# Softmax denominators of a second attention, inverted as 128 x 32 between two transfers, and another hand-over to the expert mixture

## The chip, the cores and the metric

The kernel runs on one core of one Trainium2 chip. The metric is the device time of one execution in microseconds (us). Before the change it is 692.34 us, the median of 3 runs (692.29 to 694.89).

## The reference, cut to what matters

The program is two gated blocks over x of shape (32, 64, 256): attention and feed-forward with 2:4 sparsity, then a second attention and a mixture of eight experts. The change is in the second attention and at its border with the mixture. In numpy-like words, per batch of 64 channels and 256 positions:

```
xn  = layernorm(x)                                  # over 256
qh, kh, vh = xn, ctx, ctx reshaped to (8 heads, 8 channels, 256)
qk  = einsum('bhdq,bhdl->bhql', qh, kh) / sqrt(8)   # 256 x 256 per head
ret = einsum('bhql,bhdl->bhdq', softmax(qk, -1), vh)
x   = x + tanh(g_xattn[1]) * gamma * ret
xn  = layernorm(x)
x   = x + tanh(g_ffn[1]) * (shared_expert(xn) + top2_of_8_experts(xn))
```

The softmax is written as exp(qk - max), its sum over l (the denominator), and one division of the mixed values by that sum. The mixture begins with `xn @ W_router` in plain float32, which chooses the experts.

## The kernel before, in words

`attention1` holds the second attention. x is cut into 16 tiles of 128 rows (two batches of 64 channels); a tile has 16 units (2 batches x 8 heads) of 8 channels. Five engine programs run side by side. Each calls `run_steps` with a function `step(s)`: step s works on several tiles, each at another stage: tile v = s-1 (scores and their row maxima), t = s-2 (transposed scores, exponentials, weighted sums), o = s-3 (the last quarter of the weighted sums, the denominators, the residual), and on VectorE (DVE) also p = s-4 (layernorm statistics of the new x). The first steps are written out, the middle is a hardware loop of two steps, the rest is written out; `LAG` (3) says how many steps come after the last tile has begun.

Within a step, TensorE (PE) goes through units u = 0 to 15. Each unit writes transposed scores of tile t into one of three banks `st_ps` (line 1312) and scores of tile v into one of three banks `s_ps` (line 1317). ScalarE (ACT) takes the exponential of each `st_ps` bank (L1215); DVE takes the maximum over each row of each `s_ps` bank (`TENSOR_REDUCE`, L1387). PE can begin unit u only when the bank of unit u-3 has been read. Weighted sums (`products`, L1270) go to `pv_ps`, and ACT copies them by quarters of a tile into `pv` (L1200). In `pv`, each group of 32 partitions holds, per unit, 8 rows of weighted values and on row 8 the denominators, because the value matrix `vt` has a column of ones.

At u = 5 and 7 PE multiplies `pv` by two 0/1 matrices (`selected`, L1285): `sel_out` collects the value rows into channel order, and `sel_den` copies each denominator row onto the 8 channels of its unit. ACT copies both halves, 128 x 512, into `back` (L1227, at u = 8). DVE inverts `back[:, 1]`, 128 x 256, in two halves of 128 columns (L1393, at u = 10 and 12). GpSimd (POOL) multiplies by the inverse and adds to x (L1172, L1174). DVE takes statistics (L1398).

The maxima go another way: DVE negates them, PE turns them (`turn`, L1254, at u = 2 for tile t and u = 11 for tile v), ACT copies (`a_neg_t`, L1194), and a DMA of 8 KB from SyncE's (SP's) queue puts them into the operands (`maxima`, L1095). SP's queue also carries the context tile (L1113), the operand loads (`load_operands`, L254 and L261), and the raw expert weights (L1080 to L1088), in the order of `step`. POOL prepares the next queries, splits expert weights and issues the stores of the queries (L219).

After the steps PE transposes the first four normalized tiles for the mixture (`turned.transpose`, L276), ACT copies and rounds them (L281, L286), and DVE forms their low parts (`turned.low`, L291). At the end of a block each engine drains and all meet at a barrier; in the trace this carries the line of the block's `ExitStack` (L667 for the end of the first feed-forward, L975 for the end of `attention1`). `mixture1` then loads the router weights (L1511) on SP, and PE's first work is `router(0)` on them (L1562), then the transposes of group 1 (L1548) and `router(1)`.

Of the kernel before, what the change touches and what calls it, by code (L numbers as in the profile page):

```python
# [5 lines left out]
F32 = mybir.dt.float32  # L6
# [7 lines left out]
P = 128  # L14
# [945 lines left out]
def attention1(nc, sem, keep, d):  # L960
# [14 lines left out]
    with ExitStack() as ctx:  # L975
        def sb(name, shape, dt):
# [16 lines left out]
        rden = sb("a1_rden", [P, D], F32)  # L993
# [8 lines left out]
        vt_done, vt_ready, sel_done, back_ready, rden_ready, att_ready, x_ready, st_ready = (  # L1002
            sem("a1_" + n) for n in ("vt_done", "vt_ready", "sel_done", "back_ready", "rden_ready", "att_ready", "x_ready", "st_ready"))
# [13 lines left out]
        LAG = 3  # L1017
        FILL = 18
        FIRST = Step(0, 0, 1)
# [32 lines left out]

        def opposite(u):

            return u ^ 1
# [12 lines left out]
        def _(sp):  # L1068
            def load_shared():
                for m, name in enumerate(("L1_ffn_Ws_gate", "L1_ffn_Ws_up")):  # L1070
                    sp.dma_start(ws_raw[:, m], a[name].rearrange("(c p) j -> p c j", p=P)).then_inc(ws_loaded, 16)
                down = a["L1_ffn_Ws_down"]
                sp.dma_start(wsd_raw[:, 0:FULL], down[0:FULL * P].rearrange("(c p) n -> p c n", p=P)).then_inc(ws_loaded, 16)
                sp.dma_start(wsd_raw[0:LASTM, FULL], down[FULL * P:DS]).then_inc(ws_loaded, 16)

# [31 lines left out]

            def step(s):
                maxima(s.plus(-2), 1)
                v = s.plus(-1)  # L1110
                if v.inside(TILES):
                    after(sp, vt_done, v.plus(-2))
                    sp.dma_start(ctx_t[:, v.slot], dram_at(d["ctx"], v.n)).then_inc(ctx_loaded[v.slot], 16)  # L1113
                load_operands(s, 0)
                maxima(s.plus(-1), 0)
                if s.inside(TILES) and not (s.known and s.n == 0):
                    load_pieces(s)
                load_operands(s, 1)
                if s.known and s.n == 0:
                    load_pieces(s)  # L1120
                    load_shared()
# [4 lines left out]
        def _(pool):  # L1126
# [7 lines left out]
            def step(s):  # L1134
                n, l, o = s.plus(-1), s.plus(-2), s.plus(-3)
# [33 lines left out]
                if o.inside(TILES):  # L1169
                    after(pool, rden_ready, o, 2)  # L1170
                    after(pool, x_ready, o.plus(-1))
                    pool.tensor_tensor(att[:], back[:, 0], rden[:], ALU.mult).then_inc(att_ready, 1)  # L1172
                    after(pool, att_ready, o)
                    pool.tensor_tensor(at(x_all, o.n), at(x_all, o.n), att[:], ALU.add).then_inc(x_ready, 1)  # L1174
# [8 lines left out]
        def _(act):  # L1183
# [3 lines left out]
            def step(s):  # L1187
                v, t, o = s.plus(-1), s.plus(-2), s.plus(-3)
# [12 lines left out]

                if s.known and s.n == TILES + LAG - 1:
                    norm.scalar(act, EARLY)
                for u in range(UNITS):
# [39 lines left out]
        def _(pe):  # L1244
            def step(s):
                v, t, o = s.plus(-1), s.plus(-2), s.plus(-3)
# [29 lines left out]
                def selected(w_, m):  # L1276
# [3 lines left out]
                    if m == 0:  # L1280
                        after(pe, pv_ready, w_, QUADS)
# [7 lines left out]

                def keep_active(count):  # L1290

                    for c in range(count):
                        pe.matmul(pv_ps[:], lhsT=kop[0][:, c % QUADS, 0:P], rhs=kop[0][:, 0:2].rearrange("p g n -> p (g n)"),
                                  start=True, stop=True)

                for u in range(UNITS):
# [34 lines left out]
                    if u in (5, 7):  # L1331
                        selected(o, (u - 5) // 2)
                    if u == 11:
                        def before():
                            after(pe, neg_t_ready, t, 2)
                            after(pe, back_ready, o)
# [14 lines left out]
            for dc in range(DC):  # L1351
                turned.transpose(pe, first_xn, dc, s_ps[dc][:], ident)

        @block.vector
        def _(dve):
# [6 lines left out]
            def step(s):  # L1362
                v, t, o, p = s.plus(-1), s.plus(-2), s.plus(-3), s.plus(-4)
# [11 lines left out]
                if s.known and s.n == TILES + LAG - 1:  # L1375
# [6 lines left out]
                for u in range(UNITS):  # L1382
# [21 lines left out]
def mixture1(nc, sem, keep, d):  # L1404
# [7 lines left out]
    with ExitStack() as ctx:  # L1412
# [12 lines left out]
        wr = sb("m_wr", [P, DC, E], F32)  # L1425
# [44 lines left out]
        wr_loaded, consts, xn_done = sem("m_wr_loaded"), sem("m_consts"), [sem(f"m_xn_done{g}") for g in range(GROUPS)]  # L1470
# [566 lines left out]
def flamingo(nc, a, out):  # L2037
# [13 lines left out]
    with ExitStack() as ctx:  # L2051
# [43 lines left out]
        keep["turned"] = Turned(sb, sem)  # L2095
        attention1(nc, sem, keep, d)
# [27 lines left out]
```

## Time and profile before

| | |
|---|---|
| median of 3 runs | 692.34 us |
| profiled execution, its own time | 690.52 us |
| its span, first to last instruction | 688.6 us |
| PE busy / weight loads | 599.5 us (87%) / 455.9 us (66%) |
| DVE busy | 507.8 us (74%) |
| ACT busy | 404.8 us (59%) |
| POOL busy | 315.0 us (46%) |
| second attention | from 259 to 500 us |
| mixture | from 500 us to the end |

Busy time counts instructions in execution; matmul ends are modelled, so PE's share is not PE at its peak. The granted clock ("PEclk") is that of TensorE: 1.00 is 2.4 GHz, 0.50 is 1.2 GHz. Times in a timeline are us from the span's start.

### The profile page before, as it was taken

Reading aid. Unit: us, or ns where it says so; the run is one execution under the profiler, and the core shown is the slowest. Engines: PE = TensorE matmul, PEld = TensorE weight load, DVE = VectorE, ACT = ScalarE, POOL = GpSimd, SP = SyncE. Lnnn points to the kernel's source line nnn. Section 1 sums busy time; section 2 is a strip of 40 time slices with the busy share of each in tenths; the row PEclk is TensorE's granted clock in tenths of the full one; section 3 lists DMA queues with packets and bytes.
Section 4 is the critical chain, followed back from the end, with each engine's and each line's share of the span. In section 5 each row is a group of like instructions: output and inputs, shape, how many; then the busy total and the mean of one; then the engine's idle time right before and its main releaser. Section 6 shows DMA issues by size and latency. Waiting matters only on the chain. (4 is left out here: it accounts for less than half of the span.)

```text
span 688.6 us, 16656 instructions
## 1 busy us (share of the span) xinstructions
PE 599.5 (87%) x4987; PEld 455.9 (66%) x4987; DVE 507.8 (74%) x1013; ACT 404.8 (59%) x829; POOL 315.0 (46%) x432
## 2 busy tenths in 40 slices
PE   4688878999999957999899899989579789999994
PEld 2577756788888855554455445444268679999873
DVE  2878885688887978689999999997536744444656
ACT  3888883444434423688888888888635235555431
POOL 2455554233322549556656565562144534124254
PEclk9999998999999985999999999999859999999999
DMA  5434449200000025334444433440001335456344
GB/s 162 114 102 129 122 122 314 93 1 1 0 0 1 24 70 169 101 111 140 121 118 124 132 114 113 133 121 28 1 0 50 125 96 184 147 149 189 123 137 124
DMA packets 68640, 70.70 MB, mean 103 GB/s; under 512 B 8404, under 2 KB 64852, under 8 KB 68596
## 3 DMA queue, kind: packets, MB, share of 16 engines
q1 hardware_dynamic: 63364, 55.84, 27.2%
q0 software_dynamic: 5232, 14.29, 6.7%
q8 instruction: 25, 0.41, 0.2%
q14 instruction: 19, 0.16, 0.1%
HBM read 38.48 MB, written 31.36 MB: 101 GB/s over the span
## 5 line engine op out<-in xcount | busy, mean ns | idle before, releaser
L1387 DVE TENSOR_REDUCE a_smax<-a_s 128x2 f32<-128x512 f32 x256 | 163.4, 677 | 13.9 <-PE a_s L1317 11.6
L1215 ACT ACTIVATE a_prob<-a_st 128x512 f32<-128x512 f32 x256 | 141.8, 596 | 37.3 <-PE a_st L1312 36.1
L1312 PEld LDWEIGHTS a_st<-qop,kop 64*128 64x128 f32 x512 | 70.8, 187 | 70.0 <-DVE a_smax L1387 40.8
L1312 PE MATMUL a_st<-qop,kop 64*128 64x256 f32 x512 | 104.2, 315 | 12.8 <-DVE a_smax L1387 12.8
L1317 PE MATMUL a_s<-kop,qop 64*128 64x256 f32 x512 | 106.5, 324 | 5.8 <-DVE a_smax L1387 3.6
L1270 PE MATMUL a_pv<-a_prob,a_vt 128*32 128x256 f32 x1024 | 81.6, 391 | 3.1 <-ACT a_pv_sb L1200 1.5
L819 POOL TENSOR_TENSOR f_hs_lo<-f_kept,f_hs_hi 128x512 fp32r<-128x512 f32 x32 | 41.3, 1323 | 85.6 <-ACT f_hs_hi L769 85.6
L1317 PEld LDWEIGHTS a_s<-kop,qop 64*128 64x128 f32 x512 | 73.0, 193 | 8.0 <-DVE a_smax L1387 4.9
L1832 POOL DMA_INDIRECT sorted_rows<-m_xn,m_slot x32 | 33.0, 1031 | 48.5 <-PE m_gu L128 25.9
L126 PE MATMUL f_bank<-f_xt_hi,w_hi 128*128 128x512 f32 x128 | 51.1, 400 | 1.2 <-DVE w_raw L865 0.6
L127 PE MATMUL f_bank<-f_xt_lo,w_hi 128*128 128x512 f32 x128 | 50.6, 395 | 0.0
L128 PE MATMUL f_bank<-f_xt_hi,w_lo 128*128 128x512 f32 x128 | 50.5, 394 | 0.0
L787 ACT ACTIVATE f_mag<-w_raw 128x512 f32<-128x512 f32 x32 | 20.2, 633 | 44.7 <-DVE w_raw L865 44.7
L126 PE MATMUL f_bank<-wd_hi,f_hs_hi 128*128 128x256 f32 x128 | 37.4, 292 | 6.3 <-POOL f_hs_lo L819 6.2
L1848 POOL DMA_INDIRECT m_xn<-expert_rows,m_slot x16 | 15.7, 984 | 55.0 <-DMA expert_rows<-turned 40.2
L1172 POOL TENSOR_TENSOR a_att<-a_back,a_rden 128x256 f32<-128x256 f32 x16 | 11.6, 727 | 57.8 <-DVE a_rden L1393 57.8
L865 DVE TENSOR_TENSOR w_raw<-f_sg,f_bank 128x512 f32<-128x512 f32 x32 | 21.9, 685 | 21.5 <-ACT f_sg L783 15.6
L127 PE MATMUL f_bank<-wd_lo,f_hs_hi 128*128 128x256 f32 x128 | 37.0, 289 | 0.0
L128 PE MATMUL f_bank<-wd_hi,f_hs_lo 128*128 128x256 f32 x128 | 36.9, 288 | 0.0
L1270 PEld LDWEIGHTS a_pv<-a_prob,a_vt 128*32 128x32 f32 x1024 | 20.6, 108 | 21.9 <-ACT a_pv_sb L1200 3.8
L1393 DVE RECIPROCAL a_rden<-a_back 128x128 f32<-128x128 f32 x32 | 29.9, 938 | 6.9 <-ACT a_back L1227 6.9
L783 ACT ACTIVATE f_sg<-f_bank 128x512 f32<-128x512 f32 x32 | 18.8, 586 | 27.0 <-PE f_bank L128 27.0
(260 smaller groups left out, 1663.4 us busy)
## 6 DMA issues: line engine op xcount, KB each, us to landing
qop<-qop_rows SPq DMA_DIRECT2D x64, 100.0 KB
kop<-kop_rows SPq DMA_DIRECT2D x64, 96.0 KB
sorted_rows<-x_all SPq DMA_DIRECT2D x2, 2944.0 KB, 15.4
qop<-sorted_rows SPq DMA_DIRECT2D x46, 128.0 KB, 2.3
expert_rows<-turned SPq DMA_DIRECT2D x46, 128.0 KB
kop_rows<-k_hi SPq DMA_DIRECT2D x32, 128.0 KB, 2.3
qop_rows<-q_hi POOLq DMA_DIRECT2D x30, 128.0 KB, 2.7
x_all<-in_x SPq DMA_DIRECT2D x4, 512.0 KB, 5.4
```

The costliest lines, as they stand in the source:

```text
L126: pe.matmul(out, lhsT=lh, rhs=rh, start=first, stop=False, **kw)
L127: pe.matmul(out, lhsT=lh, rhs=rl, start=False, stop=False, **kw)
L128: return pe.matmul(out, lhsT=ll, rhs=rh, start=False, stop=last, **kw)
L819: pool.tensor_tensor(hs[1][:, j], kept[:, j], raw(hs[0][:, j]), ALU.subtract).then_inc(hs_ready, 1)
L865: dve.tensor_tensor(hid[:, c, j], sg[:, j % 2], u_ps[j % 2][:], ALU.mult).then_inc(hid_ready, 1)
L1215: act.activation(prob[:, u % 8], st_ps[BANK[u]][:], ACT.Exp, scale=SCALE1).then_inc(prob_ready, 1)
L1270: mm = pe.matmul(pv_ps[v4 * 32:(v4 + 1) * 32, 0:D], lhsT=vt[:, w_.slot, c, u], rhs=prob[:, u % 8, c * D:(c + 1) * D], start=(c == 0), stop ...
L1312: st = pe.matmul(st_ps[BANK[u]][:, c * D:(c + 1) * D], lhsT=kop[t.slot][rows, u // 2, c * P:(c + 1) * P], rhs=qop[t.slot][rows, u // 2], s ...
L1317: sm = pe.matmul(s_ps[BANK[u]][:, c * D:(c + 1) * D], lhsT=qop[v.slot][rows, w // 2, c * P:(c + 1) * P], rhs=kop[v.slot][rows, w // 2], st ...
L1387: dve.tensor_reduce(smax[:, v.slot, opposite(u)], s_ps[BANK[u]][:].rearrange("p (q n) -> p q n", q=2), AX_X, ALU.max).then_inc(smax_ready, 1)
L1393: dve.reciprocal(rden[:, cols], back[:, 1, cols]).then_inc(rden_ready, 1)
L1832: pool.indirect_dma_start(out=d["sorted"][b], out_offset=bass.IndirectOffsetOnAxis(ap=slot[:, k, t:t + 1], axis=0), in_=xn[:, t], in_offse ...
```

## The change

- `back[:, 1]` is no longer inverted. Once `pv` of tile o is complete, a DMA (`spread`) takes its four denominator rows (4 partitions x 1024) to `den`, 128 partitions x 32. DVE inverts that in one instruction at u = 9 into `inverse`, and a second DMA (`collect`) writes the inverses over the denominator rows of `pv`. Both are issued on SP.
- `selected`, the copy to `back` and POOL's two instructions move one step later, to tile s-4; POOL multiplies by `back[:, 1]` as it comes. The statistics move to tile s-5, and `LAG` is 4.
- The last tile takes no transfers: its denominators go through `selected` as before, and DVE itself inverts 128 x 256, multiplies, adds and takes statistics.
- `turned.low` moves behind the statistics of the last tile. PE runs `WARM` = 10 matmuls of 512 columns without use after the transposes.
- The router weights are loaded in step 0 of `attention1`, behind the shared weights.

```diff
+        den = sb("a1_den", [P, UROWS], F32)
+        inverse = sb("a1_inverse", [P, UROWS], F32)
-        LAG = 3
+        LAG = 4
+        DRAIN = TILES + 2
+        WARM = 10
+        def last(t):
+            return t.known and t.n == TILES - 1
 # sync: load_shared, and the step
+                sp.dma_start(keep["wr"][:], a["L1_ffn_W_router"].rearrange("(c p) e -> p c e", p=P)).then_inc(keep["wr_loaded"], 16)
+            def den_rows(w_):
+                return pv[D1:P:UROWS, w_.slot].rearrange("p q n -> p (q n)")
+            def spread(o):
+                if o.inside(TILES) and not last(o):
+                    after(sp, pv_ready, o, QUADS)
+                    after(sp, inverse_ready, o.plus(-1))
+                    sp.dma_start(den[:], den_rows(o)).then_inc(den_spread[o.slot], 16)
+            def collect(o):
+                if o.inside(TILES) and not last(o):
+                    after(sp, inverse_ready, o)
+                    sp.dma_start(den_rows(o), inverse[:]).then_inc(inverse_stored[o.slot], 16)
             def step(s):
                 maxima(s.plus(-2), 1)
+                spread(s.plus(-3))
                 v = s.plus(-1)
...
                 load_operands(s, 0)
+                collect(s.plus(-3))
                 maxima(s.plus(-1), 0)
 # gpsimd
-                if o.inside(TILES):
-                    after(pool, rden_ready, o, 2)
-                    after(pool, x_ready, o.plus(-1))
-                    pool.tensor_tensor(att[:], back[:, 0], rden[:], ALU.mult).then_inc(att_ready, 1)
+                if p.inside(TILES) and not last(p):
+                    after(pool, back_ready, p)
+                    after(pool, x_ready, p.plus(-1))
+                    pool.tensor_tensor(att[:], back[:, 0], back[:, 1], ALU.mult).then_inc(att_ready, 1)
 # scalar
-                    if u == 8 and o.inside(TILES):
-                        after(act, sel_done, o)
-                        after(act, att_ready, o.plus(-1))
+                    if u == 8 and p.inside(TILES):
+                        after(act, sel_done, p)
+                        after(act, att_ready, p.plus(-1))
 # tensor: selected, the step, the end
-                        after(pe, pv_ready, w_, QUADS)
+                        if last(w_):
+                            after(pe, pv_ready, w_, QUADS)
+                        else:
+                            after_dma(pe, inverse_stored, w_)
+                        after(pe, back_ready, w_.plus(-1))
-                        selected(o, (u - 5) // 2)
+                        selected(p, (u - 5) // 2)
+            pe.wait_ge(pv_ready, TILES * QUADS)
+            keep_active(WARM)
 # vector
-                    if u in (10, 12) and o.inside(TILES):
-                        cols = slice((u - 10) // 2 * P, (u - 8) // 2 * P)
-                        after(dve, back_ready, o)
-                        after(dve, att_ready, o.plus(-1))
-                        dve.reciprocal(rden[:, cols], back[:, 1, cols]).then_inc(rden_ready, 1)
-                    if u == 2 and s.known and s.n == TILES + LAG:
-                        turned.low(dve, FIRST)
+                    if u == 9 and last(s.plus(-4)):
+                        o = s.plus(-4)
+                        after(dve, back_ready, o)
+                        after(dve, x_ready, o.plus(-1))
+                        dve.reciprocal(ctx_t[:, 0], back[:, 1]).then_inc(inverse_ready, 1)
+                        after(dve, inverse_ready, o)
+                        dve.tensor_tensor(att[:], back[:, 0], ctx_t[:, 0], ALU.mult).then_inc(att_ready, 1)
+                        after(dve, att_ready, o)
+                        dve.tensor_tensor(x_all[:, o.n], x_all[:, o.n], att[:], ALU.add).then_inc(x_ready, 1)
+                    elif u == 9 and o.inside(TILES) and not last(o):
+                        after_dma(dve, den_spread, o)
+                        after_dma(dve, inverse_stored, o.plus(-1))
+                        dve.reciprocal(inverse[:], den[:]).then_inc(inverse_ready, 1)
                     if u == 3 and p.inside(TILES):
                         after(dve, x_ready, p)
                         dve.bn_stats(at(norm.stats, p.n), at(x_all, p.n)).then_inc(st_ready, 1)
+                    if u == 4 and last(p):
+                        turned.low(dve, FIRST)
 # mixture1, sync
-            sp.dma_start(wr[:], a["L1_ffn_W_router"].rearrange("(c p) e -> p c e", p=P)).then_inc(wr_loaded, 16)
```

## Rows read from the trace of the kernel before

**Rows 1.** Busy time by stretch, one stretch of the second attention (columns as named)
```profile
core 0: us, PE busy (x) PEld busy (x) DVE busy (x) ACT busy (x) POOL busy (x), PEclk, DMA share, GB/s
404.00:417.00 13.00, 12.02 (x150) 6.58 (x150) 12.21 (x22) 10.75 (x24) 7.96 (x14) 1.00 0.41 119
```

**Rows 2.** Waits, 300 to 470 us: total us, times, longest
```profile
PE a_st L1312 <- DVE a_smax L1387: 11.5, 13, 1.0
DVE a_smax L1387 <- PE a_s L1317: 4.9, 13, 0.4
```

**Rows 3.** Groups of instructions, 240 to 490 us: busy us, mean ns, idle before
```profile
L1387 DVE TENSOR_REDUCE a_smax<-a_s 128x2 f32<-128x512 f32 x256 | 163.4, 677 | 13.9 <-PE a_s L1317 11.6
L1393 DVE RECIPROCAL a_rden<-a_back 128x128 f32<-128x128 f32 x30 | 28.1, 940 | 6.9 <-ACT a_back L1227 6.9
```

**Rows 4.** Timeline of PE, one tile: start us, us, idle before in brackets
```profile
408.80 0.38 PE L1312 MATMUL a_st<-qop,kop 64*128 64x256 f32 x1 [0.90 <-DVE a_smax L1387]
...
409.81 0.38 PE L1312 MATMUL a_st<-qop,kop 64*128 64x256 f32 x1
...
422.23 0.38 PE L1312 MATMUL a_st<-qop,kop 64*128 64x256 f32 x1 [0.92 <-DVE a_smax L1387]
```

**Rows 5.** Timeline of DVE in the same tile
```profile
418.70 0.93 DVE L1393 RECIPROCAL a_rden<-a_back 128x128 f32<-128x128 f32 x1
```

**Rows 6.** Timeline of ACT in the same tile, the last quarter of `pv`
```profile
413.10 0.39 ACT L1200 ACTIVATE a_pv_sb<-a_pv 128x256 f32<-128x256 f32 x1
```

**Rows 7.** Timeline of SP's issues in the same tile
```profile
413.39 0.36 SPq L1113 DMA_DIRECT2D a_ctx<-in_ctx  x1
...
419.58 0.53 SPq L1095 DMA_DIRECT2D qop<-a_neg_t  x1
```

**Rows 8.** DMA issues of the program: KB each, median us to landing
```profile
qop_rows<-q_lo POOLq DMA_DIRECT2D x15, 128.0 KB, 3.8
m_wr<-in_L_ffn_W_router SPq DMA_DIRECT2D x1, 8.0 KB, 1.7
```

**Rows 9.** Timeline of the end of the second attention and the mixture's start
```profile
489.03 1.07 PE L1270 MATMUL a_pv<-a_prob,a_vt 128*32 128x256 f32 x16 [0.65 <-ACT a_pv_sb L1200]
...
490.54 0.23 DVE L162 RECIPROCAL ln_rstd<-ln_std 128x12 f32<-128x12 f32 x1 [3.17 <-ACT ln_std L171]
...
490.83 0.64 PE L1285 MATMUL a_misc<-a_pv_sb,sel_out 128*32 128x256 f32 x8 [0.72 <-ACT a_pv_sb L1200]
...
491.96 0.60 ACT L1227 ACTIVATE a_back<-a_misc 128x512 f32<-128x512 f32 x1 [1.19 <-PE a_misc L1285]
...
492.64 1.75 DVE L1393 RECIPROCAL a_rden<-a_back 128x128 f32<-128x128 f32 x2
...
494.97 1.90 DVE L291 TENSOR_TENSOR turned_lo<-turned,turned_hi 128x512 fp32r<-128x512 f32 x2 [0.59 <-ACT turned_hi L286]
495.27 1.05 POOL L1174 TENSOR_TENSOR x_all<-x_all,a_att 128x256 f32<-128x256 f32 x1
496.80 0.41 DVE L1398 BATCH_NORM_STATS2 stats<-x_all 128x6 f32<-128x256 f32 x1
...
502.12 3.55 PE L1562 MATMUL m_gu<-m_wr,turned 128*128 128x8 f32 x16 [8.58 <-DMA m_wr<-in_L_ffn_W_router]
```

**Rows 10.** POOL's DRAIN at the end of the second attention: ns, start us
```profile
L975 POOLq DRAIN  x1: 4545/4545/4545, 495.5 to 495.5; - x1
```

**Rows 11.** POOL's DRAIN at the end of the first feed-forward
```profile
L667 POOLq DRAIN  x1: 2057/2057/2057, 253.0 to 253.0; - x1
```

**Rows 12.** Timeline around that end: POOL's last work, the next block's first
```profile
252.46 2.55 POOL L819 TENSOR_TENSOR f_hs_lo<-f_kept,f_hs_hi 128x512 fp32r<-128x512 f32 x2 [2.01 <-ACT f_hs_hi L769]
...
259.17 1.08 DVE L1358 BATCH_NORM_STATS2 stats<-x_all 128x6 f32<-128x256 f32 x3 [0.53 <-PEq L667]
259.17 0.70 PE L1317 MATMUL a_s<-kop,qop 64*128 64x256 f32 x6 [2.23 <-PEq L667]
```

**Rows 13.** Busy time and PEclk of two stretches at the lower clock
```profile
502.10:505.50 3.40, 3.38 (x16) 3.40 (x17) 0.70 (x3) 0.00 (x0) 3.40 (x7) 0.50 0.00 0
259.76:263.20 3.44, 0.44 (x2) 0.33 (x2) 2.90 (x12) 0.30 (x1) 3.44 (x4) 0.50 0.81 217
```

**Rows 14.** Timeline of PE later in the mixture: a router group at PEclk 1.00
```profile
521.75 1.85 PE L1562 MATMUL m_gu<-m_wr,turned 128*128 128x8 f32 x16
```

More of the change, by code:

```diff
@@ L1001, in attention1 @@
         st_done, prob_ready, pv_done, pv_ready = (sem("a1_" + n) for n in ("st_done", "prob_ready", "pv_done", "pv_ready"))
-        vt_done, vt_ready, sel_done, back_ready, rden_ready, att_ready, x_ready, st_ready = (
-            sem("a1_" + n) for n in ("vt_done", "vt_ready", "sel_done", "back_ready", "rden_ready", "att_ready", "x_ready", "st_ready"))
+        vt_done, vt_ready, sel_done, back_ready, inverse_ready, att_ready, x_ready, st_ready = (
+            sem("a1_" + n) for n in ("vt_done", "vt_ready", "sel_done", "back_ready", "inverse_ready", "att_ready", "x_ready", "st_ready"))
+        den_spread, inverse_stored = [[sem(f"a1_{n}{i}") for i in range(2)] for n in ("den_spread", "inverse_stored")]
         BORROWED = 5
@@ L1134, in step @@
             def step(s):
-                n, l, o = s.plus(-1), s.plus(-2), s.plus(-3)
+                n, l, p = s.plus(-1), s.plus(-2), s.plus(-4)
                 m = s.plus(1)
@@ L1168, in step @@
                         pool.tensor_tensor(lo, src, raw(hi), ALU.subtract).then_inc(shared_lo, 1)
-                if o.inside(TILES):
-                    after(pool, rden_ready, o, 2)
-                    after(pool, x_ready, o.plus(-1))
-                    pool.tensor_tensor(att[:], back[:, 0], rden[:], ALU.mult).then_inc(att_ready, 1)
-                    after(pool, att_ready, o)
-                    pool.tensor_tensor(at(x_all, o.n), at(x_all, o.n), att[:], ALU.add).then_inc(x_ready, 1)
+                if p.inside(TILES) and not last(p):
+                    after(pool, back_ready, p)
+                    after(pool, x_ready, p.plus(-1))
+                    pool.tensor_tensor(att[:], back[:, 0], back[:, 1], ALU.mult).then_inc(att_ready, 1)
+                    after(pool, att_ready, p)
+                    pool.tensor_tensor(at(x_all, p.n), at(x_all, p.n), att[:], ALU.add).then_inc(x_ready, 1)
             run_steps(pool, step, TILES, LAG, 2)
@@ L1187, in step @@
             def step(s):
-                v, t, o = s.plus(-1), s.plus(-2), s.plus(-3)
+                v, t, o, p = s.plus(-1), s.plus(-2), s.plus(-3), s.plus(-4)
                 def maxima_copied(w_, h):
@@ L1200, in weighted @@
                         act.activation(pv[:, w_.slot, q], pv_ps[:, 0:D], ACT.Copy).then_inc(pv_ready, 1)
-                if s.known and s.n == TILES + LAG - 1:
+                if s.known and s.n == DRAIN:
                     norm.scalar(act, EARLY)
@@ L1244, in _, with keep_active @@
         def _(pe):
+            def keep_active(count):
+                for c in range(count):
+                    pe.matmul(pv_ps[:], lhsT=kop[0][:, c % QUADS, 0:P], rhs=kop[0][:, 0:2].rearrange("p g n -> p (g n)"),
+                              start=True, stop=True)
             def step(s):
-                v, t, o = s.plus(-1), s.plus(-2), s.plus(-3)
+                v, t, o, p = s.plus(-1), s.plus(-2), s.plus(-3), s.plus(-4)
                 def turn(w_, h, before):
@@ L1288, in selected @@
                         mm.then_inc(sel_done, 1)
[L1290 to L1294, printed above, removed]
                 for u in range(UNITS):
@@ L1335, in before @@
                             after(pe, neg_t_ready, t, 2)
-                            after(pe, back_ready, o)
+                            after(pe, back_ready, p)
                         turn(v, 0, before)
@@ L1374, in step @@
                 negated(t, 1)
-                if s.known and s.n == TILES + LAG - 1:
+                if s.known and s.n == DRAIN:
                     dve.wait_ge(st_ready, EARLY.stop)
@@ L1423, in mixture1 @@
         tp_ps, down_ps = [xt_ps, ht_ps], y_ps
-        wr = sb("m_wr", [P, DC, E], F32)
+        wr, wr_loaded = keep["wr"], keep["wr_loaded"]
         xn = sb("m_xn", [P, TILES, D], F32)
@@ L1468, in mixture1 @@
         expert_f = sb("m_expert_f", [1, PART_TILES], F32)
-        wr_loaded, consts, xn_done = sem("m_wr_loaded"), sem("m_consts"), [sem(f"m_xn_done{g}") for g in range(GROUPS)]
+        consts, xn_done = sem("m_consts"), [sem(f"m_xn_done{g}") for g in range(GROUPS)]
         tp_done, plain_ready, gxthi_ready, gxt_ready, logit_done = (
@@ L2095, in flamingo @@
         keep["turned"] = Turned(sb, sem)
+        keep["wr"], keep["wr_loaded"] = sb("wr", [P, DC, E], F32), sem("wr_loaded")
         attention1(nc, sem, keep, d)
```

3 lines of the change are left out of this document (1 added, 2 removed).

## The prediction

> **What bounds the kernel now.** I first read the busy time by stretch. In 13 us of the second attention PE is busy 12.02 us and DVE 12.21 us, at PEclk 1.00 [rows 1]: two engines nearly full, so the question is which one ends each wait. The waits answer it: between 300 and 470 us PE stands still for DVE's maxima 13 times, about once per tile, 11.5 us in total, or 0.88 us each; DVE stands still for PE's scores 13 times as well, 4.9 us in total [rows 2]. The reader is to see that the bound changes sides inside a tile. Where DVE waits, PE is the bound. The timeline shows where PE waits: always before one unit, at 408.80 and again at 422.23, with 0.90 and 0.92 us of idle time [rows 4]. The time between them, 13.4 us, is one tile. That place lies just behind the two reciprocals; the first of them begins at 418.70 [rows 5], the second after two more maxima. The reciprocals cost 0.94 us each, two per tile [rows 3]. So DVE bounds a short piece of each tile, through the reciprocals, and PE the rest.
>
> Then I read the hand-over. The last products are issued at 489.03, the last copy to `back` at 491.96, DVE ends at 496.80 + 0.41 = 497.21, and PE's first work in the mixture starts only at 502.12, released by the router's load [rows 9]. Between 497.2 and 500.3 nothing computes. POOL's last work ends at 495.27 + 1.05 = 496.3 [rows 9], but its DRAIN runs from 495.5 for 4.545 us, to 500.0 [rows 10]. That DRAIN is what the barrier waits for. At the end of the first feed-forward, where POOL had issued no transfers, its last work ended at 252.46 + 2.55 = 255.0 [rows 12] and the DRAIN at 253.0 + 2.06 = 255.1 [rows 11], so nothing was added there, and the next block began 0.53 us after DVE's last instruction [rows 12].
>
> **The loop, part by part.** Removed from DVE: 2 x 0.94 = 1.88 us per tile. Added: one reciprocal of 32 columns. The nearest row is one of 12 columns, 0.23 us [rows 9]; the other bound is a 128-column one, 0.94. I take 0.25. DVE's load of 12.21 per 13.0 us is 12.6 per 13.4; it falls by 1.6 to 11.0 us.
> PE's gap goes with it, since DVE is ahead of PE everywhere else. What is late next is PE itself: 13.4 - 0.88 = 12.5 us per tile. In that time ACT has 10.75 x 13.4 / 13 = 11.1 us to do, which still fits. The lower bound of the gain is 0, if another engine holds the same place; the upper is 0.9. I take 0.88.
> The new waits:
> - `spread` waits on SP for the last quarter of `pv`, which ACT ends at 413.10 + 0.39 = 413.5 [rows 6]. The context load now issued at 413.39 [rows 7] goes behind it, by less than 1 us, and PE needs that only at u = 14. With an issue of some 0.5 us, as the 0.53 of the other small one [rows 7], the transfer starts at about 413.6. DVE reads it at u = 9, one maximum before the place of the old reciprocal: 418.70 - 0.65 = 418.05 [rows 3, 5]. It has about 4.5 us. The nearest transfers land in 1.7 us (8 KB in short runs) and 3.8 us (128 KB among others) [rows 8]. I take 2.5: hidden.
> - `collect` waits on SP for the inverse, at about 418.3, and is issued by 418.9. Behind it in the queue stand the maxima of tile v, issued at 419.58 [rows 7]: not delayed. PE wants the result at u = 5 of the next step, some 7 us later.
> - Those maxima are the nearest thing to a new bound. PE's first unit of a tile stood 1.0 us behind its gap, at 409.81 [rows 4], so at 423.24 for this tile, and will stand at 422.35. The transfer, issued from 419.58 and landing in about 1.7 to 2.2 (estimate from the 8 KB row [rows 8]), arrives at 421.3 to 421.8. 0.5 to 1.0 us is left of the cover.
> - POOL and the matmuls of `selected` only move by a step; their count is the same.
>
> The Trainium skill, page "DMA: Bandwidth & Descriptors", sections "Specifications" and "Anatomy of one DMA", speaks against such pieces: under 512 bytes a write becomes read-modify-write, and each transfer pays about 2 us fixed. By this page the two transfers cost some 4 us of latency per tile, and the sum stays, because they lie beside other work. The 8 KB load, whose runs are 32 bytes, landed in 1.7 us [rows 8], so this trace shows no more than the fixed part.
>
> Tiles concerned: the gap appears while maxima of tile v are being taken and reciprocals of tile v-2 run, that is in steps 3 to 16, 14 times. 14 x 0.88 = 12.3 us. Steps 17 and 18 are held by ACT and PE, and lose nothing.
> The first steps: one 8 KB load more on SP in step 0 (0.4 us of issue), in front of a context and an operand load. 0 to 0.4 us; I take 0.
>
> **The hand-over.** From the last products, which PE ends at 490.1 [rows 9]: `selected` of tile 14 follows without the old wait of 0.72 for ACT, two groups of 0.53, to 491.2; ACT's copy 0.6, to 491.85; `selected` of tile 15 waits for it, to 493.0; copy, to 493.6. Before, the copy of tile 15 ended at 492.56 [rows 9]: 1.05 us are lost. Then DVE takes the statistics of tile 14 (0.4) first, inverts 256 columns in 1.75 [rows 9], multiplies and adds (0.4 each, by the row of the statistics; POOL's 1.05 is the other bound, with 0.15 for each hand-over), takes statistics 0.41, and forms two low parts, which took 1.90 beside POOL's addition [rows 9] and which I take at 1.3 without it. 493.95 + 1.75 + 1.1 + 0.5 + 1.3 = 498.6. DVE thus ends 1.4 us later than at 497.2.
> POOL, on the other hand, is done with tile 14 at about 493.6, so its DRAIN, 3.7 us behind its last work as now, ends at 497.3 and hides. The barrier follows DVE by 0.5 [rows 12]: 499.1, in place of 500.3. PE starts at once, since the router weights are there; now it starts at 502.12. The gain at PE is 3.0 us. If the low parts still take 1.9 and the additions more, it is 2; if they end early, 3.5. The WARM matmuls run at 494.1 to 496.3 beside DVE and cost nothing.
>
> **The clock.** Today PEclk is 0.50 while the mixture begins [rows 13]; the router's 16 matmuls take 3.55 us there [rows 9] and 1.85 at 1.00 [rows 14]. Two router groups and the transposes between them would give back about 4.3 us at the higher level. PE's idle time before `router(0)` shrinks from 8.58 to about 2.9 us, with WARM ahead of it. But a gap of 2.23 us at the end of the feed-forward [rows 12] was followed by the lower level too [rows 13]. I take the clock as unchanged.
>
> The Trainium skill, page "TensorE: Matmul & The Clock Gate", section "HAM oscillation — how this bites in real kernels", has a gap's length decide whether the clock falls, and the new gap would be short enough for it to stay at 1.00; the sum would then be 4.3 us lower. The trace does not agree with that for the 2.23 us gap. It is the first rival below.
>
> **The sum.** 690.52 (the profiled execution's own time) - 12.3 - 3.0 = 675.2. That execution lies 1.8 below the median of 692.34; against the median it is 677.0, and this I predict.
>
> **The rivals.**
> - *The clock stays up over the hand-over*: 677.0 - 4.3 = 672.7. For it: the short gap and the dense matmuls in front. Against: the 2.23 us gap. 0.20.
> - *PE does not take all of the gap*: the maxima arrive late at the tile's first unit, or the banks make DVE, PE and ACT wait for each other in turn, and half of 12.3 is left: 683.2; at worst nothing, 689. For it: only 0.5 to 1.0 us of cover. Against: PE is already the bound in the rest of the tile [rows 2]. 0.17.
> - *POOL's DRAIN is not tied to its last work* and ends as late as now; DVE's longer end comes beside it, only the router load is saved (1.7): 678.5 to 680. 0.06.
> - *Slower: DVE waits for `spread`*. One mechanism: the transfer of 128-byte pieces lands late behind other traffic; DVE stands at u = 9, `collect` leaves late, and SP issues the maxima behind it late. Up to 4.5 us of landing nothing is lost; SP has about 0.8 more before the maxima slip and 0.6 are left after that, so from 5.9 us each us costs PE one per tile. The gain of 0.88 and the 3.0 of the hand-over are gone from 7.0 us on. At 7.5: 14 x (1.6 - 0.88) - 3 = +7: 699. Against: 3.8 is the longest of the two rows [rows 8]. 0.05.
>
> **How the numbers follow.** Forecast 0.52, whose own range is 674 to 680; rivals 0.20, 0.17, 0.06, 0.05. The range that leaves out at most 2 in 10 goes from the first rival with a little more gain to half of the second: 671.5 to 684. No change is within 0.5%, or 3.5 us, about what a measurement of this kernel can tell. Faster: 0.90; same 0.05 (the worst part of the second rival); slower 0.05.
>
> **What would show it.** Right: the reciprocals at about 0.25 us; PE's gap of 0.9 before the 15th unit gone and tiles 12.5 us apart; no wait of DVE at u = 9; POOL's DRAIN over before DVE's last instruction; `router(0)` 10 us after the last products instead of 13. Wrong: a new wait of PE at a tile's first unit (maxima), or of DVE before its reciprocal (`spread`), tiles still 13 us apart, or a DRAIN of POOL that ends after DVE. The clock: PEclk at `router(0)` and 1.85 or 3.55 us for its matmuls.

## The result, and the profile after

The changed kernel takes 675.94 us (median of 4 runs, 673.21 to 677.56); the kernel before, run beside it, takes 692.32 (691.9 to 694.89). The ratio is 0.9746 [0.9707, 0.9785]: 2.5% faster. Forecast were 677.0 us, within 671.5 to 684. The profiled executions took 690.52 and 673.21 us, 17.3 apart.

The busy times of the span of the changed kernel (share of the span, instructions):

```profile
PE 603.9 (90%) x4997; PEld 460.1 (69%) x4997; DVE 489.4 (73%) x999; ACT 404.1 (60%) x829; POOL 313.0 (47%) x430
```

DVE has lost 18.4 us of work. PE has 4.4 more, the ten matmuls of `WARM` among them (2.5 us, below), in a span 17.1 us shorter.

**In the loop.** Busy time of the same 13 us as in [rows 1] (PE, PE's weight loads, DVE, ACT, POOL, PEclk, DMA share, GB/s), then the waits from 300 to 460 us, which answer to [rows 2]:

```profile
404.00:417.00 13.00, 12.87 (x160) 6.96 (x162) 11.86 (x21) 11.63 (x27) 7.91 (x13) 1.00 0.45 135
...
DVE a_smax L1420 <- PE a_s L1348: 7.1, 25, 0.4
...
PE a_st L1343 <- DVE a_smax L1420: 0.2, 1, 0.2
```

PE is busy 12.87 of 13 us where it was 12.02, and its wait for the maxima has shrunk from 11.5 us in 13 waits to 0.2 in one. DVE now waits for PE 25 times instead of 13: PE alone is the bound, in the whole tile.

The new steps on SP and DVE in one tile (answering to [rows 5, 7]), and the next `spread`:

```profile
405.51 0.59 SPq L1125 DMA_DIRECT2D a_den<-a_pv_sb  x1
...
409.99 0.34 DVE L1434 RECIPROCAL a_inverse<-a_den 128x32 f32<-128x32 f32 x1
...
410.36 0.61 SPq L1131 DMA_DIRECT2D a_pv_sb<-a_inverse  x1
411.60 0.55 SPq L1104 DMA_DIRECT2D qop<-a_neg_t  x1
...
417.87 0.59 SPq L1125 DMA_DIRECT2D a_den<-a_pv_sb  x1
```

`spread` is issued 4.5 us before DVE needs it, and the reciprocal carries no wait in brackets. From one `spread` to the next it is 12.36 us here, and 12.40 on average from tile 0 to tile 14 (293.98 to 467.63); before, a tile took 13.4. How long the transfer takes shows only for tile 14, where DVE has nothing else to do and stands waiting; `spread` was issued at 467.63 there:

```profile
469.66 0.35 DVE L1434 RECIPROCAL a_inverse<-a_den 128x32 f32<-128x32 f32 x1 [4.75 <-DMA a_den<-a_pv_sb]
```

So DVE could read it 2.0 us after the issue. In the loop that leaves some 2.5 us of cover.

**At the hand-over.** Timeline of the end of the second attention and the mixture's start (start, duration, idle before in brackets), answering to [rows 9], and POOL's DRAIN, answering to [rows 10]:

```profile
476.34 1.07 PE L1303 MATMUL a_pv<-a_prob,a_vt 128*32 128x256 f32 x16 [0.66 <-ACT a_pv_sb L1227]
477.20 0.64 PE L1322 MATMUL a_misc<-a_pv_sb,sel_out 128*32 128x256 f32 x8
...
479.82 0.72 POOL L1201 TENSOR_TENSOR x_all<-x_all,a_att 128x256 f32<-128x256 f32 x1
...
480.20 0.60 ACT L1254 ACTIVATE a_back<-a_misc 128x512 f32<-128x512 f32 x1 [1.27 <-PE a_misc L1322]
...
481.28 1.73 DVE L1426 RECIPROCAL a_ctx<-a_back 128x256 f32<-128x256 f32 x1
481.60 2.54 PE L1275 MATMUL a_pv<-kop 128*128 128x512 f32 x10
...
484.30 1.28 DVE L291 TENSOR_TENSOR turned_lo<-turned,turned_hi 128x512 fp32r<-128x512 f32 x2
...
486.06 1.92 PE L1601 MATMUL m_gu<-wr,turned 128*128 128x8 f32 x16 [1.92 <-PEq L975]
...
490.63 3.58 PE L1601 MATMUL m_gu<-wr,turned 128*128 128x8 f32 x16 [0.69 <-ACT turned L1775]
494.35 0.22 DVE L1949 COPY m_logit<-m_gu 128x64 f32<-128x64 f32 x1 [6.00 <-PE m_gu L1601]
```
```profile
L975 POOLq DRAIN  x1: 4220/4220/4220, 480.1 to 480.1; - x1
```

DVE ends at 485.58; POOL's DRAIN is over at 484.3, 3.8 us behind POOL's last work (3.7 before), and now hidden. `router(0)` starts 9.72 us after the last products, before 13.09. It takes 1.92 us in place of 3.55, since the clock is still up:

```profile
486.06:487.98 1.92, 1.92 (x17) 1.83 (x17) 1.85 (x10) 0.30 (x1) 1.85 (x11) 0.97 0.00 0
488.00:490.60 2.60, 1.95 (x8) 1.54 (x8) 0.32 (x2) 1.19 (x2) 2.60 (x6) 0.50 0.00 0
```

PEclk (third number from the end) falls to 0.50 as `router(0)` ends, and `router(1)` takes 3.58 as before.

**The sum of the two profiles.** From the first statistics of the second attention to the last products: 489.03 - 259.17 = 229.86 before, 476.34 - 258.81 = 217.53 after, so 12.3 us less. From the last products to the first copy of the router's result: 22.85 before (that copy is at 511.88), 18.01 after, 4.8 less. The part ahead of the second attention is 0.4 us shorter, which no edit asks for. 12.3 + 4.8 + 0.4 = 17.5 of 17.3; the rest of the mixture is 0.4 longer.

### The profile page after: what moved, and what is told of

It reads as the page before. It is cut to its first block and busy times, and to the rows that moved or that the text cites. A ratio compares the mean times of both kernels' runs of the same rounds, so it can differ in the third digit from the quotient of the medians.

```text
span 671.5 us, 16680 instructions
## 1 busy us (share of the span) xinstructions
PE 603.9 (90%) x4997; PEld 460.1 (69%) x4997; DVE 489.4 (73%) x999; ACT 404.1 (60%) x829; POOL 313.0 (47%) x430
## 5 line engine op out<-in xcount | busy, mean ns | idle before, releaser
L1420 DVE TENSOR_REDUCE a_smax<-a_s 128x2 f32<-128x512 f32 x256 | 164.7, 681 | 19.9 <-PE a_s L1348 15.1
L1242 ACT ACTIVATE a_prob<-a_st 128x512 f32<-128x512 f32 x256 | 141.8, 597 | 23.8 <-PE a_st L1343 22.7
L1181 POOL TENSOR_TENSOR we_lo<-we_raw,we_hi 128x176 f32 (+3 forms) x24 | 16.5, 688 | 61.5 <-DMA qop<-qop_rows 57.6
L783 ACT ACTIVATE f_sg<-f_bank 128x512 f32<-128x512 f32 x32 | 18.7, 585 | 27.0 <-PE f_bank L128 27.0
L440 POOL TENSOR_TENSOR k_lo<-ctx_t,k_hi 128x256 fp32r<-128x256 f32 x16 | 11.7, 729 | 47.2 <-ACT k_hi L496 34.9
```

The lines of the kernel that those rows point to most:

```text
L1242: act.activation(prob[:, u % 8], st_ps[BANK[u]][:], ACT.Exp, scale=SCALE1).then_inc(prob_ready, 1)
L1420: dve.tensor_reduce(smax[:, v.slot, opposite(u)], s_ps[BANK[u]][:].rearrange("p (q n) -> p q n", q=2), AX_X, ALU.max).then_inc(smax_ready, 1)
```

## The experiments

They ran on three chips, on which the kernel before took 703.1, 699.9 and 691.9 us; so I compare ratios to the kernel before on the same chip. 0.001 is 0.7 us. Each edit is to the changed kernel, except for `e2_before_no_recip`. In each profile I measured the two stretches of the sum above, "loop" (first statistics to last products) and "hand-over" (last products to the router's copy). Before: 229.9 and 22.9; changed: 217.5 and 18.0. These two stretches can be compared between chips. The changed kernel and the runs e3 and e5 to e12 give ten profiles of nearly the same loop, and it takes 216.5 to 219.2 us in them, on all three chips. These 2.7 us are also how far a single profile of the loop can be trusted. What differs between the chips stands behind the router's copy: from there to the end of the program it is 177 to 179 us on the fastest chip, and 183 to 191 on the other two.

### DVE's two reciprocals put back

```diff
# e1_two_recips, vector
+                    if u in (10, 12) and o.inside(TILES):
+                        dve.reciprocal(spare[:, (u - 10) // 2 * P:(u - 8) // 2 * P], ident[:])
```

> The changed kernel with two more reciprocals of 128 x 128 on DVE per tile, at u = 10 and 12, of a constant into a tile that nobody reads. Theory (the loop gained by DVE's time alone): PE's gap of about 0.9 us per tile returns before the 15th unit, tiles are 13.4 us apart again or up to 0.35 more, since the small reciprocal stays: 675.9 + 12.3 = 688 us, at most 693. Rival (the gain came from the route: the results no longer pass through the copy to back before DVE, and the residual has a step more of time): the time stays within 2 us of 676.

Measured: ratio 1.0032 [1.0005, 1.006], 20 us slower than the changed kernel. The busy times of 13 us and the wait of PE, from 300 to 470 us:

```profile
326.00:339.00 13.00, 11.86 (x149) 6.49 (x148) 12.20 (x22) 10.64 (x24) 7.94 (x15) 1.00 0.40 125
...
PE a_st L1344 <- DVE a_smax L1421: 13.9, 13, 1.1
```

These are the rows of the kernel before again [rows 1, 2]: PE 11.9 of 13, DVE 12.2, thirteen waits of PE. The loop takes 493.35 - 260.03 = 233.3 us, 15.8 more; all of its gain hangs on 1.9 us of DVE per tile, though the new reciprocal, the transfers and the new order are all in. It is even 3.5 us longer than before, and its waits are 1.07 us each instead of 0.88; the small reciprocal, which stays, is the likely reason. The other 4.6 us lie in the hand-over (22.6): four of the added reciprocals, 3.5 us, fall to DVE after the last products and hold the barrier (`router(0)` 12.8 us behind the products instead of 9.7), and `router(0)` then runs at half clock, 3.55 us. The expectation had at most 17 us in all: the loop's 15.8 lies within that, but the hand-over was not in it.

### The kernel before without its reciprocals

```diff
# e2_before_no_recip, vector and gpsimd of the kernel before
-                    if u in (10, 12) and o.inside(TILES):
-                        ...
-                        dve.reciprocal(rden[:, cols], back[:, 1, cols]).then_inc(rden_ready, 1)
-                    after(pool, rden_ready, o, 2)
-                    pool.tensor_tensor(att[:], back[:, 0], rden[:], ALU.mult).then_inc(att_ready, 1)
+                    after(pool, back_ready, o)
+                    pool.tensor_tensor(att[:], back[:, 0], back[:, 1], ALU.mult).then_inc(att_ready, 1)
```

> The kernel before, with the reciprocals of the second attention left out: POOL multiplies by the denominators themselves, so this part of the softmax is not computed. Theory: the PE gap vanishes without any of the transfers, tiles 12.4 us apart, 14 x 0.9 = 12.5 us, and the last tile's 1.75 us of reciprocals go from the chain to the end of the block: 692.3 - 14.3 = 678 us. The DRAIN of POOL still ends 3.7 us behind its last addition. Rival (the transfers and the later step bring a part of the gain): 684 or more.

Measured: ratio 0.9815 [0.9772, 0.9858], -12.8 us. Loop 217.9, as in the changed kernel; its waits, and POOL's DRAIN:

```profile
PE a_st L1312 <- DVE a_smax L1387: 0.4, 1, 0.4
...
L975 POOLq DRAIN  x1: 4220/4220/4220, 483.2 to 483.2; - x1
```

The loop's 12.0 us (229.9 - 217.9) come without any transfer and without the later step, where 12.5 were expected; the two experiments close on each other from both sides. The DRAIN is over at 487.4, nothing computes until 487.6, and `router(0)` waits for its load: the reciprocals at the end are gone, but the hand-over (20.7) does not get the rest of the gain.

### The transfers taken out

```diff
# e3_no_transfers: spread and collect issue nothing, DVE inverts a constant tile
-                    sp.dma_start(den[:], den_rows(o)).then_inc(den_spread[o.slot], 16)
-                    sp.dma_start(den_rows(o), inverse[:]).then_inc(inverse_stored[o.slot], 16)
-                        after_dma(dve, den_spread, o)
-                        after_dma(dve, inverse_stored, o.plus(-1))
-                            after_dma(pe, inverse_stored, w_)
+                            after(pe, pv_ready, w_, QUADS)
```

> The changed kernel without both transfers: DVE inverts a constant tile, selected reads the denominators as they are, so the inverses do not reach the result. Theory (the transfers are hidden): within 1 us of the changed kernel, 676. Rival (SP's order or the DMA engines are loaded by them, tiles are held by late operands): faster by 2 us or more, tiles under 12.3 us apart.

Measured: ratio 0.9757 [0.9708, 0.9806], the changed kernel's own 0.9746. Loop 216.7 against 217.5. Thirty transfers of 16 KB cost 0.9 us in these two profiles, less than the 2.7 us by which the loop differs between executions, and nothing that the ratio can tell.

### The spread behind other loads

```diff
# e4_spread_late, sync
             def step(s):
                 maxima(s.plus(-2), 1)
-                spread(s.plus(-3))
...
                 load_operands(s, 0)
+                spread(s.plus(-3))
                 collect(s.plus(-3))
```

> The changed kernel with spread issued behind the first operand loads, 3.5 us later on SP. The slack is measured by this. By the trace of the changed kernel the transfer is issued at 405.5, and DVE reads it at 410.0; it takes about 2.0 us. Issued at 409.1 it lands at 411.2: DVE waits about 1.1 us at u = 9, collect leaves late, the maxima behind it slip by 0.5 us. Theory (three banks and the cover of the maxima take that): 0 to 0.3 us per tile, 676 to 680. Rival (DVE's wait goes to PE in full): 14 x 1.1 = 15 us, 691.

Measured: ratio 1.0802 [1.0737, 1.0867], 8% slower than before. This missed both expectations. One tile's issues on SP and DVE's reciprocal; then the waits from 300 to 560 us; then busy times of 170 and of 13 us:

```profile
353.32 0.82 SPq L254 DMA_DIRECT2D kop<-kop_rows  x2
354.26 0.65 SPq L261 DMA_DIRECT2D qop<-qop_rows  x2
355.11 0.62 SPq L1125 DMA_DIRECT2D a_den<-a_pv_sb  x1
...
358.18 0.35 DVE L1434 RECIPROCAL a_inverse<-a_den 128x32 f32<-128x32 f32 x1 [2.25 <-DMA a_den<-a_pv_sb]
...
377.05 0.35 DVE L1434 RECIPROCAL a_inverse<-a_den 128x32 f32<-128x32 f32 x1 [4.14 <-DMA a_den<-a_pv_sb]
...
DVE a_inverse L1434 <- DMA a_den<-a_pv_sb: 46.6, 14, 4.7
PE a_st L1343 <- DVE a_smax L1420: 35.7, 13, 3.7
...
300.00:470.00 170.00, 143.47 (x1350) 73.15 (x1350) 102.02 (x181) 104.35 (x216) 73.69 (x124) 0.76 0.30 89
339.00:352.00 13.00, 12.34 (x84) 6.11 (x88) 8.24 (x15) 6.77 (x13) 3.26 (x5) 0.50 0.22 66
```

`spread` leaves behind the operand loads and DVE can read it 3.1 us after the issue (in the tile after, issued at 372.77, 4.3). DVE stands for 3.3 us per tile and PE for 2.75 (35.7 / 13). That would make tiles of 15.1 us; they are 18.7 on average (the reciprocals of thirteen tiles begin between 300.83 and 525.36). The other 3.6 us are PE working at a lower clock: PEclk is 0.76 over 170 us, and 0.50 in stretches in which PE is busy 12.34 of 13 us. In the kernel before and in the changed kernel it is 1.00 in the loop. The waits alternate from tile to tile and reach 3.65 us, so 2.75 is a mean. A stretch at half clock passes for a full PE in the share of busy time; the number of matmuls in it (84 instead of some 160) shows the difference.

### The border with the mixture

Two kernels change only how many matmuls without use stand ahead of the barrier (`WARM` is 10 in the changed kernel); beside them runs the changed kernel itself, unedited.

```diff
# e6_warm0                      # e7_warm16
-        WARM = 10              -        WARM = 10
+        WARM = 0               +        WARM = 16
```

> The changed kernel once more, beside the kernel before in the same rounds, as the base of the three that follow. Expected: the ratio of 0.975 again, within 0.003.

> The changed kernel with WARM = 0. Theory (the ten matmuls hold the clock over the border): PE then stands still from its last transpose (481.8 in the trace of the changed kernel) to 486.1, the granted clock falls to 0.50 before router(0), whose 16 matmuls take 3.55 us in place of 1.92: slower by 1.6 us, at most 3. Rival (the clock falls anyway, as the forecast had it): no difference, and 3.55 in both.

> The changed kernel with WARM = 16. Six more matmuls of 0.22 us end at 485.4, just before DVE (485.6), so they cost nothing. Theory: PE's gap at the border shrinks from 1.9 to 0.7 us and the lower clock comes later, behind router(1), whose matmuls then take 1.9 in place of 3.6 us: up to 2.5 us faster. Rival (the router's matmuls of 8 columns let the clock fall whatever stands ahead of them): no difference within 0.5 us.

Measured, 5 rounds each: changed 0.9737 [0.9701, 0.9773], `WARM` 0: 0.976 [0.9731, 0.9788], 16: 0.9766 [0.9726, 0.9806]. The three can't be told apart; the 1.6 us that one of the expectations gave for `WARM` 0 are within these intervals. `router(0)` in the repeated changed kernel, with `WARM` 0 and with 16:

```profile
486.81 2.68 PE L1601 MATMUL m_gu<-wr,turned 128*128 128x8 f32 x16 [1.91 <-PEq L975]
```
```profile
487.23 3.55 PE L1601 MATMUL m_gu<-wr,turned 128*128 128x8 f32 x16 [4.21 <-PEq L975]
```
```profile
488.62 2.08 PE L1601 MATMUL m_gu<-wr,turned 128*128 128x8 f32 x16 [0.57 <-PEq L975]
```

Without WARM the clock had fallen already (3.55 us). With 16, PE stands for only 0.57 us, yet the clock falls at 490.2, and `router(1)` again takes 3.58: the matmuls without use do not keep it up. The six more end before the barrier does (`router(0)` starts 9.7 us behind the last products in all three), so they cost nothing and win nothing over ten. No run shows a gain of `WARM` that is clear of the noise.

Next, the last tile's multiplication and addition go back from DVE to POOL, behind DVE's reciprocal:

```diff
# e8_pool_last, vector and gpsimd
-                        dve.tensor_tensor(att[:], back[:, 0], ctx_t[:, 0], ALU.mult).then_inc(att_ready, 1)
-                        dve.tensor_tensor(x_all[:, o.n], x_all[:, o.n], att[:], ALU.add).then_inc(x_ready, 1)
+                if last(p):
+                    after(pool, inverse_ready, p)
+                    ...
+                    pool.tensor_tensor(att[:], back[:, 0], ctx_t[:, 0], ALU.mult).then_inc(att_ready, 1)
+                    pool.tensor_tensor(at(x_all, p.n), at(x_all, p.n), att[:], ALU.add).then_inc(x_ready, 1)
```

> The changed kernel with the multiplication and addition of the last tile on POOL again; DVE still inverts. Theory (the barrier waits for POOL's DRAIN, which ends 3.7 to 3.8 us after POOL's last work in a block with POOL's transfers): the addition ends at about 484.8, the DRAIN at 488.5, the mixture starts at 488.8 in place of 485.9: slower by 2.7 us, about 678.6. Rival (the DRAIN ends at the same time whatever POOL does last): slower by at most 0.7, the longer two instructions.

Measured: 0.9809 [0.9775, 0.9844], 5 us slower than the changed kernel beside it. POOL's last work, its DRAIN and `router(0)`:

```profile
486.15 0.72 POOL L1207 TENSOR_TENSOR x_all<-x_all,a_att 128x256 f32<-128x256 f32 x1
...
L975 POOLq DRAIN  x1: 4218/4218/4218, 486.4 to 486.4; - x1
...
491.07 3.55 PE L1603 MATMUL m_gu<-wr,turned 128*128 128x8 f32 x16 [4.67 <-PEq L975]
```

The DRAIN ends at 490.6, 3.7 us behind POOL's last work at 486.9, and it alone holds the barrier, since DVE ended at 488.5. The DRAIN moves with POOL's last instruction. `router(0)` starts 12.5 us behind the last products instead of 9.7: 2.8 us later, where the expectation had 2.7. The difference of the two ratios, 0.0072, is larger, but their intervals leave some 3.5 us of doubt, and in this profile `router(0)` also runs at half clock throughout.

Then two kernels undo the border in part. The first keeps only the loop's change (`WARM` 0, the last tile on POOL as in e8, and the router weights loaded by the mixture); the second only moves the router weights back:

```diff
# both: the sync programs of attention1 and mixture1 (e10_late_router has this alone)
-                sp.dma_start(keep["wr"][:], a["L1_ffn_W_router"]...).then_inc(keep["wr_loaded"], 16)
+            sp.dma_start(wr[:], a["L1_ffn_W_router"]...).then_inc(wr_loaded, 16)
```

> The changed kernel with the three edits of the border undone: router load in the mixture, WARM = 0, last tile multiplied and added on POOL. What is left is the loop. Theory (loop and border add up): the last products come 12.7 us earlier than before, as in the changed kernel; from there to the first router logits on DVE it takes 22.3 us as with the last tile on POOL alone, plus 1.7 for the load, some 24, against 22.9 before and 18.0 to 18.6 in the changed kernel. In all 5 to 6 us slower than the changed kernel, ratio to before about 0.983. Rival (the border's edits bring nothing that the mixture does not wait for anyway): 0.975.

> The changed kernel with the router load back at the start of the mixture. Theory: PE waits for it at router(0), 1.65 us and the issue, and since PE then stands still for 3.7 us the clock may fall before it: 1.7 to 3.4 us more between the last products and the logits. Rival (the transposes behind router(0) wait for DVE's normalized tiles anyway, ready 1.9 us after the start of the block): less than 1 us.

Measured: loop only 0.9832 [0.9802, 0.9863], -11.6 us; late router weights 0.9791 [0.9761, 0.9821], 3 us slower than the changed kernel. (That interval overlaps the changed kernel's, but e11 and e12 below, which ran beside it and end alike, took 674.2 to 675.9 us, and this one 677.0 to 678.5.) In the first, the hand-over takes 23.8 us, 1.0 more than before, and the loop 216.8. So the loop alone is worth 11.6 us by the ratio, and the edits of the border together some 6 (e11 and e12 below are 17.5 us faster than before), as its expectation had it. In the second, the hand-over takes 21.5 us and `router(0)` waits for its weights:

```profile
489.61 2.64 PE L1602 MATMUL m_gu<-wr,turned 128*128 128x8 f32 x16 [3.86 <-DMA wr<-in_L_ffn_W_router]
```

That is 1.9 us more of idle time than in the changed kernel, as its expectation had it (1.65 us and the issue). The other microsecond of this profile is a dip of the clock to 0.50 from 477.0 to 480.3, in which the last products took 1.93 us instead of 1.07; no edit asks for that, and I can't say that it belongs to the load.

### Where the two transfers stand in SP's queue

```diff
# e11_spread_behind_ctx: spread stands behind the context load
# e12_collect_behind:    collect stands behind maxima(s.plus(-1), 0)
```

> The changed kernel with spread issued behind the context load (128 KB) in place of ahead of it. With spread behind the operand loads (392 KB) DVE waited 3.3 us per tile and the tiles were 18.6 us apart. Theory (what counts is the time of issue and the bytes ahead in SP's queue, against some 4.5 us of cover): issued at most 0.4 us later with 128 KB ahead it lands within 3.2 us; DVE does not wait, 675 to 678 us by the ratio. Rival (any larger transfer ahead is enough): waits of DVE before the reciprocal appear, 5 us or more slower.

> The changed kernel with collect issued behind the maxima of tile v in place of ahead of them. PE reads its result some 7 us later. Theory (collect has the longest cover and the maxima did not wait for it): no difference, ratio 0.975 within 0.004. Rival (collect delays the maxima and PE's first unit): faster by 1 us or more.

Measured: 0.9748 [0.9718, 0.9778] and 0.9745 [0.9717, 0.9774], both the changed kernel's own. Either transfer can stand one place further back in the queue at no cost; it is behind the operand loads (e4) that `spread` comes too late. Both kernels, and e3 and e4, have the changed kernel's border unedited, so they also repeat its clock. `router(0)` in the two:

```profile
487.43 3.51 PE L1601 MATMUL m_gu<-wr,turned 128*128 128x8 f32 x16 [1.90 <-PEq L975]
```
```profile
485.81 3.43 PE L1601 MATMUL m_gu<-wr,turned 128*128 128x8 f32 x16 [1.90 <-PEq L975]
```

The idle time in front is the same 1.9 us, but `router(0)` runs at half clock. Over the profiles of kernels with the changed loop, from timelines and short windows (the fall of the clock is reckoned from the start of the last products):

| kernel | WARM | clock falls after | router(0) | hand-over |
|---|---|---|---|---|
| changed | 10 | 11.6 us | 1.92 us | 18.0 us |
| changed again | 10 | 10.7 | 2.68 | 18.6 |
| e3 | 10 | 9.9 | 3.37 | 19.3 |
| e4 | 10 | 10.5 | 2.80 | 18.7 |
| e11 | 10 | 9.8 | 3.51 | 19.4 |
| e12 | 10 | 9.9 | 3.43 | 19.3 |
| e6 | 0 | 9.3 | 3.55 | 19.5 |
| e7 | 16 | 11.3 | 2.08 | 18.0 |
| e8 | 10 | 10.0 | 3.55 | 22.3 |
| e9_loop_only | 0 | 9.0 | 3.55 | 23.8 |
| e10 (after the dip above) | 10 | 13.7 | 2.64 | 21.5 |

The first six rows have one and the same border. It gives anything from 18.0 to 19.4 us, as the fall of the clock comes at 9.8 or at 11.6 us. The 1.5 us that the changed kernel's first profile shows beyond the forecast thus belong to that execution and not to the kernel. In every profile, the kernel before included, `router(1)` runs at half clock (3.58 us).

## Why the prediction was right

Point by point, in its order:

- **Who bounds the loop.** Right, and shown from both sides (e1, e2): DVE bounded a short piece of each tile through the reciprocals, and PE the rest. Forecast 12.3 us, measured 12.3; that the two agree to the tenth is luck, since the other nine profiles of the loop give gains of 10.7 to 13.4 us. Tiles of 12.5 us were forecast, 12.4 measured.
- **The small reciprocal.** 0.25 taken, 0.34 measured. It costs nothing, since DVE waits for PE again.
- **The transfers.** 2.5 us of landing taken, 2.0 measured where it shows (one place, from the start of the issue); both hidden (e3). The fixed 2 us that the prediction took from the Trainium skill, page "DMA: Bandwidth & Descriptors", stand in its section "Anatomy of one DMA" for transfers that POOL issues. These two go out on SP, so the 2.0 measured here is the number to go by. What the pieces of 128 bytes cost beyond this can't be seen in any run.
- **The maxima behind `collect`** had 0.5 to 1.0 us of cover by the forecast. In the changed kernel's profile PE never waits for them from 300 to 460 us, and their place before or behind `collect` makes no difference to the time (e12). In the same stretch of five other profiles it does wait for them, once or twice in a dozen tiles and for 0.4 to 1.3 us (e5, e6, e7, e8, e11), as it does once in e2, where there is no `collect`. The cover is thin, as forecast, but the rival in which PE waits in every tile is out.
- **DVE's longer end.** 9.57 us behind the products forecast, 9.24 measured. The low parts took 1.28 (1.3 taken), the inversion 1.73 (1.75).
- **POOL's DRAIN.** Right: 3.7 us behind its last work forecast, 3.8 measured, and it moves with that work (e8). The rival in which it is not tied is out. Where it isn't hidden (e8), `router(0)` starts 2.8 us later. The hand-over is 4.3 us longer (22.3 against 18.0), but 1.6 of that is `router(0)` at half clock, which the changed border shows in some executions too; by the ratio it is 5 us, give or take 3.5.
- **`router(0)`** 3.0 us earlier forecast, 3.4 measured. Of this the early load is 1.9 (e10).
- **The clock.** "Unchanged" is right for `router(1)` and the transposes in every run, and for `router(0)` in e11 and e12, not in the changed kernel's own profile, where it gave 1.5 us. The rival in which the clock stays up over the whole hand-over (4.3 us) is out: `router(1)` takes 3.58 us in every profile, even with a gap of 0.57 us in front of `router(0)` (e7). The page "TensorE: Matmul & The Clock Gate" of the Trainium skill, section "HAM oscillation — how this bites in real kernels", has the length of PE's idle gap decide. The trace of that run does not agree: the gap was 0.57 us and the clock fell.
- **The slower rival** did not come true in the changed kernel, but e4 shows that it was sized wrongly. Its mechanism is real, but its price was read as PE's waiting time alone. Against `spread` issued 4.5 us ahead, e4 issues it some 3.5 us later (behind the loads, which end at 409.05 in the changed kernel's tile) and it is readable 1 to 2.3 us later after its issue; on the forecast's scale that is a landing of 6.6 to 7.8 us, for which it gave at most 1.9 us per tile over the changed kernel (7.8 - 5.9). Measured: 2.75 us of PE's waiting, and some 3.6 more because a lower clock came with it, together 6.3.

The sum was 12.3 + 3.0 = 15.3. The medians are 16.4 us apart, and the ratio makes 17.6 us of 692.3 [14.9, 20.3]. In the profile of e12, whose `router(0)` got nothing from the clock, it is 13.1 (476.10 - 259.31 = 216.8) + 3.5 = 16.6. What lies beyond 15.3 is a few tenths in each of the two terms and, in some executions, up to 1.5 us of clock; the interval of the ratio holds both 15.3 and 16.6, so the runs can't say more.

## What to carry to other kernels

Look for the engine that is the bound for one microsecond of each tile, not on average: taking 1.5 us of work (1.88 out, 0.34 in) from just before that wait removed the whole wait of 0.9 us, 14 times, although over the whole program the engine that did the work is busy 74% and the one that waited 87%. Work that lies across 256 columns because a matmul copied it there can be done where it is 8 times more compact, if the transfers to and from that form have a whole step to hide in and stand in their queue ahead of the large loads. At the end of a block ask which engine's last instruction the barrier waits for, DRAIN included: give the last work to the engine whose DRAIN is short.

## What the runs showed of the hardware that I had not expected

- A wait that comes back in each tile can cost more than its length. With 1.8 to 3.7 us of PE's waiting in each tile, 2.75 on average, PEclk was 0.76 on average and 0.50 for stretches in which PE had little idle time (e4, one profile): tiles took 18.7 us instead of 12.4. With 0.88 us per tile, in the kernel before, PEclk was 1.00 over the loop.
- POOL's DRAIN took 4.2 us at the end of the block in which POOL issues transfers (4.5 in the kernel before), and ended 3.7 to 3.8 us behind its last work; DVE's took 1.0 us and ACT's 1.2. In the block where POOL issued none it ended 0.1 us behind that work [rows 11, 12]. That the transfers are the reason was not tried.
- The instant at which the clock falls moves by 1.8 us between executions that do the same thing (first six rows of the table). It fell in the middle of `router(0)`, while PE was busy, in one profile of the changed kernel, and at its end in another.
